# Graph attention with LayerNorm on one core: in head 0 ScalarE's shuffling transfers ahead of its mask pieces, mask marks that wait for their own buffer, and the denominator as a tensor-scalar operation

## The reference

```python
def gnn(x, spatial, edge, Wq, Wk, Wv, Wout):         # n = 2048 tokens, d = 256, h = 8 heads
    q = (x @ Wq).reshape(h, n, d)                      # k, v alike
    a = jnp.einsum('hnd,hmd->hnm', q, k) * d ** -0.5
    a = a + spatial + edge
    mask = spatial == 0.0
    a = jax.nn.softmax(jnp.where(mask, -1000000.0, a), axis=-1)
    a = jnp.where(mask, 0.0, a)
    out = jnp.einsum('hnm,hmd->hnd', a, v).transpose(1, 0, 2).reshape(n, h * d)
    return out @ Wout

return layernorm(x + gnn(x, adj, adj, Wq, Wk, Wv, Wout))   # adj is 2048 x 2048, nearly all zero
```

## Time and profile before

| what | value |
|---|---|
| time, median of 3 runs | 1822.61 us (1822.05 to 1825.81) |
| the profiled execution | 1825.55 us, of which its span is 1823.8 us |
| busy: TensorE, its weight loads | 98%, 87% |
| busy: VectorE, GpSimd, ScalarE | 61%, 54%, 47% |
| chain that ended last | TensorE 85%, SyncE's issuing 2%, VectorE 2%, transfers 1% |

### The profile page before, as it was taken

How to read it: one execution, slowest core, us unless ns; L and a number is a source line. 1 busy time by engine, 2 the same in 40 slices (tenths; PEclk the granted TensorE clock), 3 DMA queues, 4 the chain that set the end, 5 groups by cost and what they waited for, 6 DMA issues and landing times.

```text
span 1823.8 us, 29365 instructions
## 1 busy us (share of the span) xinstructions
PE 1794.9 (98%) x10272; PEld 1582.9 (87%) x10272; DVE 1112.3 (61%) x2318; ACT 854.3 (47%) x1411; POOL 983.8 (54%) x762
## 2 busy tenths in 40 slices
PE   8999889999999999999999999999999999999998
PEld 7987779888998889988899888988889888898887
DVE  6888855555555655556554555555555556546667
ACT  5655454444454445444454444544445444544433
POOL 6888764544644555444554555644455455554443
PEclk9999999999999999999999999999999999999999
DMA  7888875666656666466665666656655566655664
GB/s 251 246 255 269 249 215 155 191 193 195 174 160 184 192 195 188 141 198 195 189 188 144 199 188 191 182 156 201 192 177 175 162 199 197 185 160 172 175 174 139
DMA packets 186995, 345.97 MB, mean 190 GB/s; under 512 B 39392, under 2 KB 96736, under 8 KB 170464
## 3 DMA queue, kind: packets, MB, share of 16 engines
q10 hardware_dynamic: 92032, 200.59, 35.2%
q1 hardware_dynamic: 94816, 143.50, 28.7%
HBM read 190.84 MB, written 18.87 MB: 115 GB/s over the span
## 4 chain that ended last, share of the span: by engine, by line
PE 85%; SPq 2%; DVE 2%; DMA 1%; issue 1%; POOL 0%; ACT 0%; ACTq 0%; DVEq 0%
PE bank L401 33%; PE y_bank L417 22%; PE bank L366 18%; PE y_bank L425 12%; SPq L305 2%; DMA p_turned<-blocks 1%; DVE blocks L666 1%; POOL p_split L483 0%; DVE y_acc L754 0%; ACTq L579 0%; PE bank L386 0%; ACT m_sb L570 0%; DVE zero_mark L702 0%; DVE small L673 0%; DVE t_p L643 0%
## 5 line engine op out<-in xcount | busy, mean ns | idle before, releaser
L483 POOL TENSOR_TENSOR p_split<-p_turned,p_split 128x512 fp32r<-128x512 f32 x510 | 649.7, 1302 | 563.1 <-ACT p_split L551 562.8
L401 PE MATMUL bank<-k_split,q_split 128*128 128x512 f32 x3072 | 789.3, 392 | 2.0 <-DVE small L643 2.0
L401 PEld LDWEIGHTS bank<-k_split,q_split 128*128 128x128 f32 x3072 | 557.2, 189 | 104.4 <-DVE small L643 3.3
L417 PE MATMUL y_bank<-v_split,p_split 128*128 128x512 f32 x2048 | 547.2, 390 | 2.4 <-ACT p_split L551 2.4
L643 DVE CUSTOM_DVE_ANT_0 t_p<-bank,m_sb 128x512 f32<-128x512 f32 x512 | 351.6, 687 | 207.2 <-PE bank L401 178.6
L417 PEld LDWEIGHTS y_bank<-v_split,p_split 128*128 128x128 f32 x2048 | 384.3, 188 | 84.5 <-ACT p_split L551 3.7
L542 ACT ACTIVATE t_p<-t_p,small 128x2048 f32<-128x2048 f32 x128 | 257.3, 2010 | 353.7 <-DVE small L655 349.4
L472 POOL TENSOR_TENSOR w_slot<-raw_w,w_slot 128x512 fp32r<-128x512 f32 x192 | 249.6, 1301 | 233.8 <-ACT w_slot L522 230.6
L551 ACT ACTIVATE p_split<-p_turned 128x512 fp32r<-128x512 f32 x512 | 288.8, 621 | 113.3 <-DMA p_turned<-blocks 109.0
L666 DVE STREAM_TRANSPOSE blocks<-t_p 128x2048 f32<-128x2048 f32 x128 | 295.8, 2311 | 61.2 <-ACT t_p L542 45.3
L366 PE MATMUL bank<-x_t,w_slot 128*128 128x256 f32 x2304 | 307.8, 285 | 11.9 <-issue 7.8
(11 more groups left out here) (44 smaller groups left out, 634.8 us busy)
## 6 DMA issues: line engine op xcount, KB each, us to landing
m_sb<-m_dram ACTq DMA_DIRECT2D x112, 1024.0 KB, 5.3
p_turned<-blocks SPq DMA_DIRECT2D x1532, 64.0 KB, 2.2
p_turned<-blocks ACTq DMA_DIRECT2D x516, 64.0 KB, 2.7
blocks<-in_adj_dram SPq DMA_DIRECT2D x64, 256.0 KB, 4.0
raw_w<-in_L_gnn_Wv_dram ACTq DMA_DIRECT2D x64, 256.0 KB, 3.5
m_dram<-m_sb SPq DMA_DIRECT2D x16, 1024.0 KB, 6.5
raw_w<-in_L_gnn_Wq_dram ACTq DMA_DIRECT2D x63, 256.0 KB, 3.4
raw_w<-in_L_gnn_Wk_dram ACTq DMA_DIRECT2D x61, 256.0 KB, 3.9
```

Source lines behind the costliest of these rows:

```text
L401: mm = nc.tensor.matmul(dst[:], q[:, a, k, f * P:(f + 1) * P], k_split[:, kk, k, b * BANK:(b + 1) * BANK], start=(i == 0), stop=(i == len( ...
L417: nc.tensor.matmul(y[:], p_split[tau % 2][:, HI, j * P:(j + 1) * P], v_split[:, j].rearrange("p s d -> p (s d)"), start=(j == 0), stop=False)
L483: nc.gpsimd.tensor_tensor(lo, p_turned[:, i * BANK:(i + 1) * BANK].rearrange("p (j b) -> p j b", b=QUAD), hi.bitcast(F32), ALU.subtract).t ...
```

## The change

There are three edits.

1. In head 0 (tau 1 to 15) ScalarE issues `shuffle(tau - 1)` at b = 1, behind the `hi_p` and ahead of `scale_mark(t + 1, 1)` and of what is due; in the other heads it stays at b = 2 but stands ahead of what is due there.
2. A mark of GpSimd's pieces waits until the last earlier mark in the same buffer has been scaled. Before, it waited for every earlier one.
3. The denominator's first operation is a `tensor_scalar` with two 128x1 scalars and one tensor. Before it was a `scalar_tensor_tensor` with two tensors and one scalar.

```diff
+        def mark_before(a):
+            earlier = [e for e in by_pool if e < a and e % BANKS % 2 == a % BANKS % 2]
+            return max(earlier) if earlier else None
...
                             hi_p(tau - 2, 2 * b)
                             hi_p(tau - 2, 2 * b + 1)
+                        if 1 <= tau <= ALL and b == (1 if tau < TILES else 2):
+                            for i in range(QUADS):
+                                shuffle(tau - 1, i)
                         if tau + 1 < TILES and b:
                             scale_mark(t + 1, b)
                         for key in due(tau, b):
...
-                        if 1 <= tau <= ALL and b == 2:
-                            for i in range(QUADS):
-                                shuffle(tau - 1, i)
...
-                    nc.vector.scalar_tensor_tensor(out=row_sum[:, t:t + 1], in0=floor_exp[:, t:t + 1],
-                                                   scalar=count[:, t:t + 1], in1=row_sum[:, t:t + 1],
-                                                   op0=ALU.mult, op1=ALU.add).then_inc(denom_ready, 1)
+                    nc.vector.tensor_scalar(row_sum[:, t:t + 1], floor_exp[:, t:t + 1], count[:, t:t + 1],
+                                            row_sum[:, t:t + 1], ALU.mult, ALU.add).then_inc(denom_ready, 1)
...
-                    if a in by_pool and by_pool[a] > 2:
-                        dve.wait_ge(m_scaled, by_pool[a] - 1)
+                    if a in by_pool and mark_before(a) is not None:
+                        dve.wait_ge(m_scaled, by_pool[mark_before(a)])
```

## The result

The changed kernel takes **1826.93 us** in the median (1825.27 to 1829.03), the kernel before on the same chip 1824.62 (1822.05 to 1826.96): a ratio of 1.0014, interval 1.0008 to 1.0020. It is slower by some 2.3 us where 4.6 less were forecast. A part of the miss in absolute time is the base: 22 runs of the kernel before have a median 2.0 above that of the three runs from which I worked. The profiled execution takes 1825.62 us, the one of before 1825.55; both spans are 1823.9 and 1823.8. So the two traces show no gain rather than the loss, and I read their stages, not their ends.

The account below looks back on a forecast made before the run. Bound: the softmax chain of head 0's early tiles, which sets when TensorE runs without gaps. Terms 1.34, 1.55, 1.05, 1.0 and -0.3 sum to 4.6 us: 1822.6 becomes 1818.0 us, range 1814.0 to 1823.0.

Parts of the forecast that it names:

- competing loops: Early tiles of head 0: the step from turn to turn is set by VectorE's own work with waits, or Loop (b).
- the rival on this: Denominator in head 0: the new form waits beside GpSimd like the old one; gain only 2.9 us, 1819.7 us, chance 0.12.
- the margin of 0.5 us: Tiles of head 0: mark q = 3 starts 3.7 us after the turn's end, its awaited scaling done by 3.2.
- the step that failed: ScalarE in head 0: four issues of 2.46 us fit where it waited anyway; the third scaled mark's 1.99 us wait goes.
- Loop (b): Single buffer in head 0: turn, 12 SyncE issues, last landing, next turn; binds nearly every tile from 4 to 11.
- The rival by which SyncE's issues are stretched: Tiles 4 to 12: ScalarE's earlier transfers cost SyncE one 1.15 us stall each; 10.4 us lost, 1828.4 us, chance 0.10.
- its weaker form: Same stretching of SyncE's issues at 0.3 us a tile over nine tiles: takes 2.7 of 4.6, 1820.7 us, chance 0.22.
- those of tiles 2, 12 and 13: Head 0 savings, each the smaller of VectorE's saving and the room: 1.34, 1.55 and 1.05 us.
- the room: Tile 2 of head 0: how much its step can shorten before Loop (b) binds, taken as 1.34 us.
- The last tile: End of head 0: key splits and weight roundings queue behind ScalarE's four issues, delaying TensorE's projection; charged 0.3 us.

Follow-up runs that it names:

- edits 2 and 3: The kernel before with the marks' new wait and the denominator's new form, ScalarE's issues where they were: 1823.11 us, 0.9988 of before; repeated, 0.9993.
- the early place with mark and splits ahead: Against edits 2 and 3, ScalarE's issues in head 0 moved to b = 1, behind the first scaled mark and due splits: 1824.66 and 1823.88 us (0.9997, 0.9996).
- the second profile: Profiled execution of the changed kernel's repeat run, nothing further changed: 1831.12 us; that run's ratio to before is 1.0014.
- the kernel with the mark first: The changed kernel with the first scaled mark moved ahead of ScalarE's four issues, the due splits still behind them: 1825.30 us, 1.0006 of before.

## Why the prediction was wrong

- **What bounds, and where head 0 ends:** right. After the wait that ends at 234.27 TensorE streams with one gap, 0.25 us ahead of the projection at 240.05, and a step of the early tiles is set by the longest of competing loops. There are three and not two.
- **The range:** it ended 0.4 above the median of three runs, one of which stood 3.2 above it. With 22 runs before is at 1824.62, so that no change at all would have come out above 1823.0 too. The direction was wrong apart from that.
- **The denominator:** 0.27 us in all 13 tiles where I took 0.17, so 0.46 saved in the median and not 0.56. It lay inside GpSimd's work in all of them and did not wait, so the rival on this falls. The Trainium skill (SBUF — State Buffer, "Who interferes with whom") has a VectorE instruction with two inputs from SBUF contend with a GpSimd instruction that reads SBUF, and a tensor_scalar only in two-port modes; the trace agrees: 0.269 to 0.274 in each tile, the old form 0.217 to 1.36.
- **The marks:** the margin of 0.5 us was not there. It rested on a mark scaled by 3.2 us after the turn's end; with issues of 3.2 to 4.1 the scaling starts at 3.3 to 4.2 and takes 0.7 more. In tiles 4, 6, 8, 10 and 12 0.43 to 0.50 us of waiting stayed, and 1.1 and 1.0 in tiles 2 and 13.
- **ScalarE's four issues: the step that failed.** "At their new place the ScalarE engine had waited for VectorE anyway" looked at ScalarE's idle time and not at what stands behind the four. I listed the third scaled mark and the split of x, and left out the query's split in six tiles and the first scaled mark's users. And their length of 2.46 came from a place where GpSimd's low parts were long done: in tile 12 of before by 207.98, ahead of issues at 210.69. In tile 11 of the changed kernel (second row) they end at 195.52, 2.5 us after the turn:

```profile
202.93 5.05 POOL L483 TENSOR_TENSOR p_split<-p_turned,p_split 128x512 fp32r<-128x512 f32 x4 [0.99 <-ACT p_split L551]
189.82 5.70 POOL L488 TENSOR_TENSOR p_split<-p_turned,p_split 128x512 fp32r<-128x512 f32 x4 [0.26 <-ACT p_split L556]
```

  At the turn's end the third and fourth are still being made, one every 1.3 to 1.4 us, and the issues are held by them. By the turns 0 to 14 edit 1 costs 5.1 to 6.9 us against edits 2 and 3, by the runs 4.3; I had charged it 0.3. Of the 4.3, 3.2 come back when the first scaled mark and the splits stand ahead; how they fall to the mark and to the query stays open.
- **Loop (b) "itself is not shortened":** true. The rival by which SyncE's issues are stretched did not happen in the changed kernel: the twelve take 83.9 and 84.6 us in sum over tiles 2 to 11, and 85.0 before. A cost of the size of its weaker form is there: I gave it 0.3 us a tile, 2.7 in all, and a chance of 0.22, and the early place with mark and splits ahead costs 3.5 us over the ten steps from turn 2 to 12, 0.35 each. But most of it lies behind the last issue and not in the issues, so that the number agrees is no proof of the mechanism.
- **The sum of edits 2 and 3:** 4.9 by my terms (4.6 and the 0.3 back), 4.3 and 4.5 by turns 0 to 14. So the terms were about right in the traces: those of tiles 2, 12 and 13 (1.34, 1.55, 1.05) measured 1.0 to 1.2, 1.3 and 0.9. The first was worked out wrongly: 81.61 + 1.4 + 0.22 is 83.2 and not 83.4, so the room was 1.5 and the sum 4.8. Yet the runs show 1.7 us. Their traces end 2.2 and 3.6 earlier than that of before. In the first, 0.6 of the 4.3 is a later turn 0, TensorE's wait at the end of head 0 ends 3.7 earlier, and the rest goes in the last tile, where TensorE stalls 0.68 us. The profile of before stood 0.9 above the median of all its runs, not 2.9.
- **The last tile:** ScalarE's splits did queue behind the issues, and TensorE had a gap of 0.25 us there for the 0.3 charged. But the second profile has 1.0 at that place, the kernel with the mark first none, and the end did not notice.

## What to carry to other kernels

Before issues of transfers are moved ahead on an engine, list everything that stands behind them until they are done, and find each wait that they carry themselves: an idle engine is only free for work that can be done at once, and an issue that waits for another engine's product ties all that is behind it to that engine. Price a moved instruction with the length that it has when its inputs are late, not with the one from its old place. And where two loops are within half a microsecond of each other, a saved wait comes back as another, so count a saving only up to the next loop, and look for that one in every engine's queue.

## Unexpected of the hardware

An issue can stall on both engines at the same moment. In tile 9 of the changed kernel the second issues of SyncE and ScalarE took 1.77 and 1.85 us, where 0.59 and 0.54 are the medians (60 to 225 us):

```profile
166.87 1.77 SPq L310 DMA_DIRECT2D p_turned<-blocks  x1
```

```profile
166.88 1.85 ACTq L584 DMA_DIRECT2D p_turned<-blocks  x1
```

In tiles 7 and 11 it was the same (1.5 and 1.6, 1.9 and 1.9). In all three SyncE had issued a store of 1 MB 2.2 to 2.6 us before its shuffle, so the two do not seem independent there; what holds them is not shown. The Trainium skill (DMA: Bandwidth & Descriptors, "Issuing engines are not separate DMA queues") says that transfers of all issuing engines run on the same 16 DMA engines and interleave, and that issuing on several saves only the sequencer's time, usually small beside the transfer. The stalls at the same moment fit the first, and no run shows more of it. The second is not small here: four issues of 0.63 more on SyncE in each of 14 tiles cost 26 us against edits 2 and 3 (1.0135 less 0.9990).
